# Self attention with its keys first, and other places for rounding, sums and stores in cross attention

## What is computed

```python
ln_out = _ln(hidden_states, ln_w, ln_b)
q = _ln(_fp8_linear_pertensor(ln_out, wq, ...).reshape(b, s, g, hpg, d), qln_w, qln_b)
k = _ln(_fp8_linear_pertensor(ln_out, wk, ...).reshape(b, s, g, d), kln_w, kln_b)
v = _fp8_linear_pertensor(ln_out, wv, ...).reshape(b, s, g, d)
core = _gqa(q, k, v).reshape(b, s, nh * d)            # self attention
qx = _ln(_fp8_linear_pertensor(ln_out, wqx, ...).reshape(b, s, g, hpg, d), qxln_w, qxln_b)
kx, vx = jnp.split(jnp.einsum('bsi,oi->bso', cond, w_kv_x), 2, axis=-1)
xout = _gqa(qx, _ln(kx...), vx...)                    # cross attention, cond is the context
catq = _div_clamp_fp8(jnp.concatenate([core, xout], -1), proj_smooth)
return jnp.einsum('bsi,oi->bso', catq, wproj) * (proj_in_scale * proj_w_scale)
```

## Time and profile before

| | |
|---|---|
| median of 3 runs | 2896.58 us (2896.07 to 2899.03) |
| profiled execution | 2896.9 us, span 2895.1 us |
| mean granted TensorE clock | 0.940 |
| TensorE busy | 2545.1 us (88%) |
| VectorE busy | 2156.1 us (74%) |
| ScalarE, GpSimd busy | 1100.6 us (38%), 928.2 us (32%) |
| stages before self attention | 0 to 1032 us |
| self attention | 1032 to about 1400 us |
| cross attention | about 1400 to 2645 us |
| stages behind it | 2645 to 2895 us |

### The profile page before, as it was taken

The page is one execution under the profiler, slowest core; times in us unless marked ns, Lnnn a source line. Parts: engine busy times, 40 slices in busy tenths (PEclk is TensorE's granted clock), DMA queues, the critical chain, the costliest instruction groups (busy, mean ns, idle before and its releaser), DMA issues. The chain is left out here.

```text
span 2895.1 us, 39559 instructions
## 1 busy us (share of the span) xinstructions
PE 2545.1 (88%) x13434; PEld 2221.3 (77%) x13434; DVE 2156.1 (74%) x3892; ACT 1100.6 (38%) x1787; POOL 928.2 (32%) x584
## 2 busy tenths in 40 slices
PE   7999999939999957777699999999999999986797
PEld 5777777738999945666588888888888888875797
DVE  8777777773333367777488889999999999993377
ACT  1000000014444445556144444545444444444332
POOL 6560000000000012443255555555555555553000
PEclk9999999969999958888799999999999999998899
DMA  6444333120111030101322122222222222213311
GB/s 240 182 172 158 137 143 135 55 73 30 59 44 44 0 115 26 39 39 39 118 73 70 62 73 73 73 73 71 70 66 68 69 69 65 65 38 86 103 50 40
DMA packets 116412, 231.89 MB, mean 80 GB/s; under 512 B 22176, under 2 KB 94704, under 8 KB 112240
## 3 DMA queue, kind: packets, MB, share of 16 engines
q1 hardware_dynamic: 112880, 218.35, 22.2%
q0 software_dynamic: 3456, 12.58, 1.1%
HBM read 158.95 MB, written 71.96 MB: 80 GB/s over the span
## 5 line engine op out<-in xcount | busy, mean ns | idle before, releaser
L1358 POOL TENSOR_TENSOR s_acc<-s_acc,s_sx 125x896 f32<-125x896 f32 x128 | 356.4, 2784 | 249.0 <-ACT s_sx L1422 248.9
L290 DVE BATCH_NORM_STATS2 s_st<-ps 125x6 f32<-125x128 f32 x1536 | 316.2, 286 | 114.2 <-PE ps L246 112.4
L1422 ACT ACTIVATE s_sx<-s_sx 125x896 f32<-125x896 f32 x192 | 184.0, 959 | 461.4 <-DVE s_sx L1574 461.3
L1505 PE MATMUL ps<-s_p_hi,s_cn_hi 125*128 125x448 f32 x768 | 297.7, 388 | 7.3 <-DVE s_p_lo L1580 6.9
L1468 PE MATMUL ps<-s_qc_hi,s_ct_hi 128*125 128x448 f32 x768 | 294.5, 383 | 1.3 <-issue 1.3
L1556 DVE TENSOR_TENSOR s_sx<-ps,keep_krs 125x896 f32<-125x896 f32 x192 | 208.7, 1087 | 106.8 <-PE ps L1468 103.2
L1468 PE MATMUL ps<-s_qc_lo,s_ct_hi 128*125 128x448 f32 x768 | 286.0, 372 | 0.0
L1468 PE MATMUL ps<-s_qc_hi,s_ct_lo 128*125 128x448 f32 x768 | 285.4, 372 | 0.0
L1505 PE MATMUL ps<-s_p_lo,s_cn_hi 125*128 125x448 f32 x768 | 283.1, 369 | 0.0
L1505 PE MATMUL ps<-s_p_hi,s_cn_lo 125*128 125x448 f32 x768 | 282.8, 368 | 0.0
L246 PE MATMUL ps<-s_wk_hi,s_hi 128*125 128x512 f32 x768 | 246.5, 402 | 40.3 <-DVE s_st L290 21.8
(11 more groups left out here) (303 smaller groups left out, 6054.9 us busy)
## 6 DMA issues: line engine op xcount, KB each, us to landing
s_raw<-in_ctxt SPq DMA_DIRECT2D x16, 1500.0 KB, 7.3
ct_hi<-s_hi SPq DMA_DIRECT2D x16, 1500.0 KB, 10.4
ct_lo<-s_lo SPq DMA_DIRECT2D x16, 1500.0 KB, 13.6
s_ct_hi<-ct_hi SPq DMA_DIRECT2D x48, 500.0 KB, 3.8
s_ct_lo<-ct_lo SPq DMA_DIRECT2D x48, 500.0 KB, 4.5
s_cn_raw<-in_ctx SPq DMA_DIRECT2D x48, 500.0 KB
s_w<-in_w SPq DMA_DIRECT2D x16, 1024.0 KB, 5.3
qx<-s_qxs SPq DMA_DIRECT2D x16, 448.0 KB, 2.8
```

The costliest lines, as they stand in the source:

```text
L290: ins = dve.bn_stats(st[:, G * t + g, :], kx[0:TT, t % NB, g // 4, DH * (g % 4):DH * (g % 4) + DH])
L1358: pool.tensor_tensor(a, a, p[:, PR * w.pt:PR * w.pt + PR, :], ALU.add).then_inc(s["acc_ready"], 1)
L1422: act.activation(p, p, ACT.Exp).then_inc(s["exp_ready"], 1)
L1505: mm = pe.matmul(pv[:, k, :], x[:, t, k * P:k * P + P], y[w.vr][:, j, :], start=(t == 0 and c == 0), stop=(t == NT - 1 and c == 2))
```

## The change

In self attention the order of the chunks becomes keys, queries, cross queries, values (`TURN_OF`, `ORDER`); the weights are loaded in that order. The scores of a pair move into its own turn (slots 7 to 10), its maxima to slots 8 to 11, and all that follows into the first slots of the next turn. Three kinds of the first input are rounded ahead of the turns, and the fourth in slots 3 and 4.

In cross attention the sums (L1528) move from the end of step 2 to step 3, between its scores and its values product. The reciprocals are split in a high and a low part (two more VectorE operations), eight unit matrices are scaled and not four, and two one-pass products take the place of the fp32 one. The values are read out at step 5 of the same unit, and rounded at step 3 of the next. On VectorE the second query residual stands ahead of step 3's scores. The stores move in SyncE's queue.

```diff
 CHUNKS = 2 * NQ + 2 * NK
 NORMED = CHUNKS - NK
-LAST = [NQ - 1, 2 * NQ - 1, 2 * NQ + NK - 1, CHUNKS - 1]
-KIND = [0] * NQ + [1] * NQ + [2] * NK + [3] * NK
+PART = [0] * NQ + [1] * NQ + [2] * NK + [3] * NK
+TURN_OF = [2, 0, 1, 3]
+ORDER = [c for part in TURN_OF for c in range(CHUNKS) if PART[c] == part]
+KIND = [TURN_OF.index(PART[c]) for c in ORDER]
+LAST = [max(c for c in range(CHUNKS) if KIND[c] == kind) for kind in range(4)]
...
-        SCORES, MAXIMA, EXPS = (0, 1, 2, 3), (1, 2, 3, 4), (5, 5, 5, 5)
-        SUMS, TURNED, VALUES, OUTPUT = (6, 7, 7, 8), (8, 9, 10, 11), (9, 10, 11, CHUNKS), (10, 11, CHUNKS, CHUNKS + 5)
-        SCALED, QUANTISED = ({}, {7: 0, 9: 1, 10: 2, 11: 3}), ({0: 3}, {8: 0, 10: 1, 11: 2})
+        SCORES, MAXIMA, EXPS = (7, 8, 9, 10), (8, 9, 10, 11), (CHUNKS,) * 4
+        SUMS, TURNED = [tuple(CHUNKS + t for t in ts) for ts in ((1, 2, 2, 3), (3, 4, 5, 6))]
+        VALUES, OUTPUT = [tuple(CHUNKS + t for t in ts) for ts in ((4, 5, 6, 7), (5, 6, 7, CHUNKS))]
+        SCALED, QUANTISED = ({3: 3}, {3: 0, 9: 1, 10: 2}), ({4: 3}, {4: 0, 10: 1, 11: 2})
...
                 def scores(q, a):
-                    if a == 0:
-                        pe.wait_ge(s["tr_read"], NORMED * q + NORMED)
+                    pe.wait_ge(s["tr_read"], NORMED * q + NK + a + 1)
...
@@ cross attention, SyncE
                     for c in range(NCH):
                         load_cn(b, c)
+                    if not first(b) and not (static(b) and b == 1):
+                        store(b - 2, 1)
                     if more:
                         load_q(b + 1)
+                        load_ct(b + 1, 0)
                     if not first(b):
                         store(b - 1, 0)
                     if more:
-                        load_ct(b + 1, 0)
                         load_ct(b + 1, 1)
-                    if not first(b):
-                        store(b - 1, 1)
-                    if more:
                         load_ct(b + 1, 2)
@@ GpSimd
-                    if w.i == 0 and w.three_back:
+                    if w.i == 3 and w.three_back:
                         d = w.u - 3
                         pool.wait_ge(s["cc_ready"], d + 1)
@@ ScalarE
                     if w.i == 3 and w.two_back:
-                        act.wait_ge(s["r4_ready"], w.u - 1)
+                        act.wait_ge(s["r4_lo_ready"], w.u - 1)
                         if not (static(b) and w.u < 3):
                             act.wait_ge(s["rb_ready"], w.u - 2)
-                        for j in range(HG):
-                            ins = act.activation(rdiag[:, j, :], keep.ident[0:PAIR, 0:PAIR], ACT.Copy, scale=r4[:, j:j + 1])
+                        for part, r in enumerate((r4_hi[:, :].bitcast(F32), r4_lo[:, :])):
+                            for j in range(HG):
+                                ins = act.activation(rdiag[part][:, j, :], keep.ident[0:PAIR, 0:PAIR], ACT.Copy, scale=r[:, j:j + 1])
                         ins.then_inc(s["rdiag_ready"], 1)
@@ TensorE
+                    if w.i == 3 and w.two_back:
+                        pe.wait_ge(s["acc_ready"], NPR * (w.u - 1))
+                        if w.one_back:
+                            pe.wait_ge(s["mt_read"], w.u)
+                        if w.new and w.next:
+                            pe.wait_ge(s["qc_lo_ready"], K2 * w.u + 2 * K2)
+                        for j in range(HG):
+                            mm = pe.matmul(sums[:, j:j + 1], acc[w.h][:, 0, PAIR * j:PAIR * j + PAIR], keep.ones[0:TT, 0:1], start=True, stop=True)
+                        mm.then_inc(s["sum_ready"], 1)
                     if w.i == 4 and w.two_back:
                         pe.wait_ge(s["rdiag_ready"], w.u - 1)
-                        if w.new and w.next:
-                            pe.wait_ge(s["qc_lo_ready"], K2 * w.u + 2 * K2)
-                        pe.matmul(misc[:, 0:QH], keep.ones[0:PAIR, :], rdiag[:, :, :], start=True, stop=True).then_inc(s["rb_ready"], 1)
+                        for part in range(2):
+                            mm = pe.matmul(misc[:, 0:QH], ones_r[:, :], rdiag[part][:, :, :], start=(part == 0), stop=(part == 1))
+                        mm.then_inc(s["rb_ready"], 1)
...
-                    if w.i == 2 and w.two_back:
-
-                        pe.wait_ge(s["acc_ready"], NPR * (w.u - 1))
-                        if w.one_back:
-                            pe.wait_ge(s["mt_read"], w.u)
-                        for j in range(HG):
-                            mm = pe.matmul(sums[:, j:j + 1], acc[w.h][:, 0, PAIR * j:PAIR * j + PAIR], keep.ones[0:TT, 0:1], start=True, stop=True)
-                        mm.then_inc(s["sum_ready"], 1)
@@ VectorE
+                    if w.i == 3 and w.next and w.new:
+                        qc_split(w.u + 1, 1 - w.h, 1)
                     if w.new:
                         dve.wait_ge(s["sc_ready"], w.n + 1)
...
-                    if w.i == 0 and w.three_back:
-                        dve.wait_ge(s["rb_read"], w.u - 2)
-                        dve.wait_ge(s["v_ready"], w.u - 2)
-                        dve.tensor_tensor(ca[:, :], misc[:, 0:QH], rsc[:, :], ALU.mult).then_inc(s["v_read"], 1)
-                        dve.wait_ge(s["v_read"], w.u - 2)
-                    if w.i in (2, 3) and w.next and w.new:
-                        qc_split(w.u + 1, 1 - w.h, w.i - 2)
+                    if w.i == 2 and w.next and w.new:
+                        qc_split(w.u + 1, 1 - w.h, 0)
...
                         dve.reciprocal(r4[:, :], sums).then_inc(s["r4_ready"], 1)
+                        dve.wait_ge(s["r4_ready"], w.u - 1)
+                        dve.tensor_copy(r4_hi[:, :], r4[:, :]).then_inc(s["r4_hi_ready"], 1)
+                        dve.wait_ge(s["r4_hi_ready"], w.u - 1)
+                        dve.tensor_tensor(r4_lo[:, :], r4[:, :], r4_hi[:, :].bitcast(F32), ALU.subtract).then_inc(s["r4_lo_ready"], 1)
...
+                    if w.i == NPR - 1 and w.two_back:
+                        dve.wait_ge(s["rb_read"], w.u - 1)
+                        dve.wait_ge(s["v_ready"], w.u - 1)
+                        dve.tensor_tensor(ca[:, :], misc[:, 0:QH], rsc[:, :], ALU.mult).then_inc(s["v_read"], 1)
...
+                    if w.i == 3 and w.three_back:
+                        dve.wait_ge(s["v_read"], w.u - 2)
+                        if not (static(b) and w.u < 4):
+                            dve.wait_ge(s["cat_ready"], w.u - 3)
+                        dve.tensor_scalar(cb[:, :], ca[:, :], FP8_MAX, -FP8_MAX, ALU.min, ALU.max).then_inc(s["cb_ready"], 1)
...
```

More of the change, by code:

```diff
@@ L785, in self_attention @@
         beyond = lambda p: isinstance(p, int) and p >= NP
[L786 removed]
+        slots = lambda p: range(max(OUTPUT) - CHUNKS + 1 if beyond(p) else CHUNKS)
         def at_slot(table, t, p, act):
             for a in range(NQ):
[L791 to L794 removed]
+                back, left = divmod(table[a] - t, CHUNKS)
+                if left == 0 and back >= 0 and not early(p, back) and not beyond(p - back if isinstance(p, int) else p):
+                    act(p - back, a)
         def input_work(table, t, i, r, act):
[L798 removed]
+            if t in table[r] and not (isinstance(i, int) and i + r >= COUPLES):
                 act(i + r, table[r][t])
@@ L880, in turn @@
                         input_work(QUANTISED, t, i, par, round_input)
-                for kind in range(4):
+                for kind in range(3):
                     round_input(0, kind)
@@ L1193, in _ @@
                     weight_lo(c)
-                for kind in range(1, 4):
+                for kind in range(1, 3):
                     quantise(0, kind)
```

70 lines of the change are left out of this document (31 added, 39 removed).

## The result

The changed kernel took 2845.8 us (2843.2 to 2850.3), the kernel before 2896.3 beside it: a ratio of 0.983 (0.981 to 0.985), a gain of some 50 us where 90 were forecast. By the first and last instructions of each stage, self attention lasted 365.9 us and lasts 332.3 (-34, forecast -28); cross attention lasted 1249.1 and lasts 1229.1 (-20, forecast -62). All that is lacking is lacking in cross attention.

What follows compares the result with a forecast made beforehand. TensorE was taken to bound cross attention, VectorE close behind, and chains between engines self attention. Cross attention -62 and self attention -28 gave -90: 2807 us, own range 2785 to 2830, widened to 2778 to 2846.

Steps and rivals of the forecast that it cites:

- L1604's successor at 0.28 us: Cross attention, VectorE: this operation, 2.08 us beside GpSimd's additions, falls to 0.28 once the rounding leaves steps 0 and 1.
- Self attention, -28: Whole stage: turns -16 from shorter seams, drain -11, start -3, first turn +2; bounds -46 and -8.
- Rival 2: Self attention doesn't gain, its seam moving whole behind ScalarE's exponentials and table loads: 2835 us, chance 0.09.
- Sums, -40 and +16: Cross attention: moving the sums to step 3 ends 40.0 us waiting for GpSimd; a late residual costs 16.
- Transposes, -25: Cross attention's seam: reading values out at step 5 removes the transposes' 24.8 us wait for the read-out.
- late seam (+16): Uncharged bound in cross attention: if the maxima L1598 and L1593 both stretch, 1 us for one unit of two.
- Reciprocals, -11: Cross attention: two one-pass products for the fp32 one save 0.35 us in each of 32 units.
- The slack of 0.8: Cross attention: time left ahead of TensorE's reciprocal product after ScalarE's added scaling, 1.0 us before; hides the scaling.
- The clock, -3: Cross attention: with the gaps gone, fewer half-clock slices on TensorE, -3 us.
- Rival 1: Shared port: GpSimd's work makes each last maximum late, the seam keeps 25 us, residual takes 3: 2835, chance 0.16.
- rival 3: Clock: a half-clock slice stays in every unit, bodies take 2.8 us more, 13 times: 2843, chance 0.07.
- Rivals 4 and 5: VectorE becomes the bound, slower, 2939, chance 0.05; TensorE's waits only change names, self attention gains nothing, 2897, chance 0.03.

Runs made afterwards that it cites:

- p3: Kernel before with only the rounding part (values read out at step 5, rounded at step 3, stores moved): 2834.9 us, ratio 0.9788.
- e2: Cross attention of the changed kernel with self attention of the kernel before: 2876.1 us, ratio 0.993.
- q2: Kernel before with the rounding part and the sums' move (TensorE's move and VectorE's order), reciprocals as before: 2860.1 us, ratio 0.9872.
- q1: Kernel before with the rounding part and the one-pass reciprocals, sums in their old place in step 2: 2850.8 us, ratio 0.9837.
- w3: Kernel before with keys first, the rounding part and VectorE's order; sums in step 2, reciprocals in one float32 product: 2793.3 us, ratio 0.9647.
- e5: Changed kernel with three quarters of GpSimd's low parts of the context rows left out from entry 2 on: 2777.7 us, ratio 0.9593.
- e3: Changed kernel with the context rows' rounding and low parts one step earlier (steps 6, 8, 10): 2819.3 us, ratio 0.9733.
- r2: Kernel before with the rounding part and VectorE's order only (second residual ahead of step 3's scaling), TensorE's sums unmoved: 2828.7 us, ratio 0.9758.

## Why the prediction was wrong, point by point

The forecast was 2807 and 2845.8 came out, at the outer edge of the range of 2778 to 2846 that rivals 1 to 3 had widened; the forecast's own range ended at 2830. Of the signs that it named, L1604's successor at 0.28 us and the seams of self attention came; a body of 70 to 71.5 us and a wait under 5 us before the transposes did not.

*Self attention, -28: right, and for its reasons.* The seams, forecast at 6.5 and 9.5 us, took 7.2 and 8.9; a pair of turns fell from 78.5 to 71.7 us, -20 for six turns where -16 stood (by the prediction's own terms, 1.9 and 5.0 less 0.5 and 1.6, it is 2.4 a turn and not the 2.7 it took, so -14); the slots gave nothing back, for the seams alone are 1.3 and 5.5 shorter. The drain, forecast at -11, is 38.5 to 27.7. The stage gave -34. Rival 2 falls.

*Sums, -40 and +16: right in the changed kernel, and worthless.* 40.0 became 13.9, -26 where -24 stood. But p3 shows that the rounding part takes the 40 away by itself, to 3.3. The prediction booked the roundings' departure from steps 0 and 1 as "1.8 us" that VectorE gets back, and used them only for the maximum. It did not follow them down the chain of the sums' own wait, where scaling, subtraction, exponential, addition and fold all come 2.6 us sooner. Two edits were given one wait each, and both could take the same one; of the two only the sums' move carries the residual's wait.

*Transposes, -25: this is the step that failed.* The prediction let the wait go since its releaser, the read-out, was moved, and noted that "what is late next is their other source, the maximum", 1.6 us ahead of the transposes by the earlier trace rows. That slack was none. The transposes started at 2073.69 after 1.58 us of idle time, so TensorE was free at 2072.11, and the maximum had ended at 2072.10: with the read-out out of the way, every further microsecond by which TensorE came sooner was a wait for the maximum. TensorE was spared its waits at the sums, while the maximum hangs on VectorE, which ran without idle time for the 16 us before, now with the read-out in that stretch. The wait came out at 34.7 (+10, not -25). The working charged nothing for it and kept a late seam (+16) for the bounds; even that was too little.

*Reciprocals, -11: right as a duration, wrong as a gain.* The product's busy time fell by 10.9. In the changed kernel a body without half clock got no shorter by it (73.55 us in e2, 73.46 in q2), the stall at the seam grew from 1.6 to 2.2 us, and 13 of 14 bodies of e2 have a stretch at half clock where q2 has none; in the place of q1 the eight diagonals were late. The slack of 0.8 held in after (0.5 us of waiting in all), so the hidden cost was not the scaling on which the prediction set it.

*The clock, -3.* The forecast was fewer half-clock stretches. Between the first body and the drain there were 5 before and are 11 after, and 6 x 1.45 is +9. The granted clock is at its lower level (1.2 of 2.4 GHz) for most of the 3.4 us that follow the 2.2 us stall. What decides whether a stretch comes is open: three bodies of after have the same stall and none, and in before waits of 1.1 to 1.5 us at the sums were followed by one in five units and by none in more than twenty. That more activity releases the clock, as the Trainium skill says (TensorE: Matmul & The Clock Gate, The HAM clock gate), agrees with p3 and w3, which have none between the first body and the drain; it gave no help in telling whether stalls would be fewer.

The sum by these rows is -26 + 10 - 11 + 9 = -18, and the stage gave -20.

*Rivals.* Rival 1, the shared port, had the mechanism at the seam: it keeps its 25 us because each last maximum is late, 2835. It came out at 35 us, and half-clock stretches as in rival 3 came on top, though one in most bodies and not two in each. That the operations stretch beside GpSimd is shown by the timeline (1.08 us alone, up to 2.93 beside it), and that this makes the seam late by e5 and e3. That the cause is the SBUF interfaces that GpSimd shares with VectorE is the rule of the Trainium skill quoted in the prediction; the runs agree with it (operations of VectorE on two SBUF inputs stretch, while L1563 and L1580, which read PSUM, stay under 1.1 beside a running addition), but none takes the port apart from other causes. Rivals 4 and 5 fall as such: the kernel is faster, and VectorE is busy 66.3 of 74.9 us. Yet locally it is the bound, in the stretch of 16 us ahead of one seam, and a share of the whole body hid that.

What stays open: whether it is the port by which the two engines hinder each other, what exactly brings a half-clock stretch, and what the pieces of the rounding part (read-out, roundings, stores) give one by one, for they were only run together.

## What to carry to other kernels

Before two edits are each given a wait, follow the wait's own chain back over every engine and ask whether one edit already shortens it; here it ran from TensorE over GpSimd and ScalarE to VectorE. A wait for an engine that has no idle time ahead of it does not go with the releaser that the profile names: what is spared elsewhere comes back there, so look at the last 10 to 20 us of each engine ahead of a seam and not at its share of the body. And take a change apart on the chip: of five pieces here (keys first, roundings, VectorE's order, TensorE's sums, reciprocals) three gave 103 us and two took back half.

## What the runs showed of the hardware that was not expected

- A stall of 2.2 us ahead of the transposes was followed by 3.4 us at a granted clock of 0.53 in 11 of 14 settled bodies, at 1.45 us each, and in 13 of 14 in e2; in q2, with 1.6 us at the same place, no settled body had one. The length of a stall alone does not settle it: waits of 1.1 to 1.5 us at the sums of before were followed by such a stretch in five units and by none in more than twenty.
- With two operands in SBUF, a VectorE operation on 125x896 elements takes 1.08 us alone; beside GpSimd's low parts or additions the same took up to 3.3, and the one on 125x448, 0.63 alone, took 2.67. With one operand in PSUM (L1563, L1580 of after) none of some 340 took over 1.10, whether GpSimd worked or not.
- A small operation can be dear by its place: moving the residual, 0.61 us, ahead of a scaling that had to wait for scores anyway was worth 0.53 us in each body, 6 us in r2, without touching any other engine.
